# Two-layer block on one core: scores and first distances in pairs, two value groups side by side, values projected into the shared bank

## The reference

```
def _stablemax3_s(x):
    pos = 1.0 + x * (1.0 + 0.5 * x * (1.0 + x / 3.0))
    neg = 1.0 / (1.0 - x * (1.0 - 0.5 * x * (1.0 - x / 3.0)))
    return jnp.where(x >= 0, pos, neg)
qkv = layernorm(x) @ w_qkv.T
attn = stablemax3(q @ k.T * scale)               # per head
x = x + (attn @ v) @ w_out.T + b_out
logits = layernorm(x) @ router_w + router_b      # top 2 of 4 kept, made to sum to 1: gates
h = silu(xf @ w1[e]) * (xf @ w3[e])
x = x + sum_e gates[e] * (h @ w2[e])
```

## Time and profile before

| | us |
|---|---|
| median of three runs (1226.88 to 1228.73) | 1228.69 |
| the profiled execution | 1225.98 |
| its span in the trace | 1224.2 |
| PE busy in the span | 1143.0 (93%) |
| VectorE busy | 1041.6 (85%) |
| ScalarE busy | 1017.0 (83%) |
| GpSimd busy | 332.1 (27%) |

### The profile page before, as it was taken

How to read it: one execution, slowest core, us unless ns; L and a number is a source line. 1 busy time by engine, 2 the same in 40 slices (tenths; PEclk the granted TensorE clock), 3 DMA queues, 4 the chain that set the end, 5 groups by cost and what they waited for, 6 DMA issues and landing times.

```text
span 1224.2 us, 29210 instructions
## 1 busy us (share of the span) xinstructions
PE 1143.0 (93%) x10116; PEld 976.4 (80%) x10116; DVE 1041.6 (85%) x1998; ACT 1017.0 (83%) x1070; POOL 332.1 (27%) x707
## 2 busy tenths in 40 slices
PE   1567999999999999999999999999999999999988
PEld 1445888888888888888888888888888888898878
DVE  5777989888898988889898888989888889998833
ACT  1488988888998888899888889898888899888872
POOL 5113322212332222233222132322312233231111
PEclk9778999999999999999999999999999999999999
DMA  5111111222111122211112121111222111121000
GB/s 175 58 57 53 48 50 57 67 66 65 46 47 48 56 65 65 65 48 44 48 56 65 65 65 51 41 48 56 65 65 65 55 43 43 56 65 62 11 6 9
DMA packets 83689, 67.97 MB, mean 56 GB/s; under 512 B 6664, under 2 KB 82120, under 8 KB 83656
## 3 DMA queue, kind: packets, MB, share of 16 engines
q1 hardware_dynamic: 83080, 67.01, 17.1%
q10 hardware_dynamic: 576, 0.52, 0.2%
HBM read 45.42 MB, written 20.97 MB: 54 GB/s over the span
## 4 chain that ended last, share of the span: by engine, by line
PE 81%; DVE 5%; issue 4%; DMA 3%; SPq 3%; ACT 2%; POOL 2%; DVEq 0%; POOLq 0%; ACTq 0%
PE up_a L807 15%; PE up_a L983 10%; PE up_b L983 10%; PE up_b L807 9%; PE sc L876 9%; PE pv L823 7%; PE sc L966 6%; PE pv L807 5%; SPq L311 2%; DVE mx L716 2%; DVE y_acc L733 1%; DMA qk_scratch<-qk_split 1%; PE misc L1014 1%; PE misc L1015 1%; PE misc L938 1%
## 5 line engine op out<-in xcount | busy, mean ns | idle before, releaser
L464 ACT ACTIVATE w_sq<-sc 128x1024 f32<-128x1024 f32 x256 | 262.6, 1026 | 140.6 <-PE sc L876 133.6
L603 DVE SCALAR_TENSOR_TENSOR poly<-w_sq,sc 128x1024 f32<-128x1024 f32 x256 | 311.5, 1217 | 34.8 <-ACT w_sq L464 25.6
L716 DVE TENSOR_REDUCE mx<-sc 128x4 f32<-128x1024 f32 x256 | 305.1, 1215 | 18.0 <-PE sc L966 17.3
L521 ACT ACTIVATE poly<-poly,two 128x2048 f32<-128x2048 f32 x128 | 251.9, 1991 | 0.4
L526 ACT ACTIVATE poly<-poly 128x2048 f32<-128x2048 f32 x128 | 242.4, 1895 | 0.0
L876 PE MATMUL sc<-q_stack,k_pad 128*128 128x256 f32 x1024 | 179.1, 298 | 7.4 <-DVE poly L603 6.9
L472 ACT ACTIVATE silu_a<-up_a 128x512 f32<-128x512 f32 x256 | 154.0, 602 | 18.9 <-PE up_a L807 14.3
L876 PEld LDWEIGHTS sc<-q_stack,k_pad 128*128 128x128 f32 x1024 | 144.1, 193 | 25.0 <-issue 13.6
L807 PE MATMUL up_a<-xn_hi,w_hi 128*128 128x256 f32 x512 | 155.9, 304 | 6.2 <-DVE y_acc L733 1.3
L966 PE MATMUL sc<-k_pad,q_stack 60*128 60x256 f32 x1024 | 117.1, 329 | 31.7 <-DMA k_pad<-qk_scratch 22.9
L381 POOL TENSOR_TENSOR x_resb<-x_res,b_out_all 128x128 f32<-128x128 f32 x64 | 27.9, 457 | 431.8 <-DVE y_acc L656 361.4
(11 more groups left out here) (105 smaller groups left out, 2021.5 us busy)
## 6 DMA issues: line engine op xcount, KB each, us to landing
qk_scratch<-qk_split SPq DMA_DIRECT2D x32, 512.0 KB, 2.8
k_pad<-qk_scratch SPq DMA_DIRECT2D x256, 64.0 KB
q_stack<-qk_scratch SPq DMA_DIRECT2D x124, 128.0 KB
x_in<-in_L_attn_x_dram SPq DMA_DIRECT2D x32, 128.0 KB, 2.1
x_res<-in_L_attn_x_dram SPq DMA_DIRECT2D x32, 128.0 KB, 2.3
out_dram<-y_acc SPq DMA_DIRECT2D x32, 128.0 KB, 1.8
poly<-in_L_ffn_w_dram SPq DMA_DIRECT2D x2, 1024.0 KB, 7.2
q_stack<-m_split SPq DMA_DIRECT2D x64, 16.0 KB
```

The lines of the kernel that those rows point to most:

```text
L464: nc.scalar.activation(w_sq[:, u % 2, :], sc[:, u % 2, :], ACT.Square).then_inc(sq_ok, 1)
L521: nc.scalar.activation(poly[:, C * g:C * (g + 1), :], poly[:, C * g:C * (g + 1), :], ACT.Ln, bias=two[:]).then_inc(ln_ok, 1)
L603: nc.vector.scalar_tensor_tensor(poly[:, u, :], w_sq[:, u % 2, :], 3.0, sc[:, u % 2, :], ALU.add, ALU.mult).then_inc(poly_ok, 1)
L716: nc.vector.tensor_reduce(by_row[:, :, 2 * g:2 * g + 2], sc[:, u % 2, :].rearrange("p (j k t) -> p j k t", j=2, k=2), AX.X, ALU.min, negat ...
```

## The change

PE's order changes in five ways. (1) The scores go in pairs, u = (0, 1), (2, 3), (4, 5), (6, 7), and the first half of `down(0)` (its rows c = 0) goes ahead of the first pair. (2) `weighted_values` 0 and 1 stand side by side behind the last scores; before, group 0 stood behind `scores(4)`. (3) `router_logits` goes from between `scores(6)` and `scores(7)` to behind `up_a_unit(0)`, which is behind `maxima_T`, and `up_b_unit(0)` and `queries_operand` go ahead of `weighted_values(2)`. (4) `distances` 0 and 1 stand side by side, `weighted_values(3)` behind them. (5) The values are projected into `misc` instead of `pv`, straight behind `weighted_values(3)`, ahead of the units 1.

VectorE follows: `route_logits` goes from ahead of `scores_max(7)` to behind `add_expert(3)`, `add_expert(1)` goes behind `scores_max(3)`, and `queries_T` goes ahead of the router's comparisons. ScalarE does `square(1)` ahead of the copy of the attention output, the copy of the values before `silu(1)`, and the router's small exponential (L548) behind `weights_of(3)` instead of ahead of it. The number and the sizes of the operations stay the same.

The core of the diff:

```
@@ scalar, first half
                 silu(0)
                 square(0)
+                square(1)
                 if has(i, off - 1):
                     nc.scalar.copy(o_T[:], pv[:]).then_inc(o_ok, 1)
-                square(1)
-                silu(1)
-                square(2)
                 if has(i, off + 1):
...
-                                              pv[:, 0, c * D:(c + 1) * D].rearrange("p (h d) -> p h d", d=HD))
+                                              misc[:, c * D:(c + 1) * D].rearrange("p (h d) -> p h d", d=HD))
+                silu(1)
+                square(2)
                 silu(2)
@@ vector, second half
-                    if u == 6 and has(i, off - 1):
-                        route_logits()
-                    if u in (1, 2) and has(i, off - 2):
-                        add_expert(u - 1)
...
+                    if u in (1, 3) and has(i, off - 2):
+                        add_expert(u // 2)
                     if u == 4 and has(i, off - 1):
                         router_T()
...
+                if has(i, off - 2):
+                    add_expert(2)
+                if has(i, off + 1):
+                    split_maxima()
+                if has(i, off - 2):
+                    add_expert(3)
+                if has(i, off - 1):
+                    route_logits()
+                if has(i, off + 2):
+                    queries_T()
@@ tensor: units 0 to 7, weighted values
-                    pe.wait_ge(v_ok, n + 2 if has(i, off + 1) else n + 1)
+                    pe.wait_ge(v_ok, n + 1)
...
-                        pe.wait_ge(v_ok, m + 4)
...
+                    pe.wait_ge(o_ok, min(m + 2, B) if isinstance(i, int) else m + 2)
@@ tensor, first half
                 distance(0)
+                distance(1)
                 if has(i, off - 1):
                     weighted_values(i, off - 1, 3)
-                distance(1)
+                if has(i, off + 1):
+                    m = n + 1
+                    pe.wait_ge(qk_out, m + 1)
+                    for c in range(C):
+                        last = nc.tensor.matmul(misc[:, c * D:(c + 1) * D], xn_T[:, c * 128:(c + 1) * 128],
+                                                proj_T[:, 2, :], start=True, stop=True)
...
@@ tensor, second half: maxima_T, queries_operand, router_logits
                     if has(i, off - 1):
-                        pe.wait_ge(lg_ok, n)
+                        pe.wait_ge(xn2_out, n)
...
-                    if has(i, off + 1):
+                    if has(i, off - 1):
+                        pe.wait_ge(lg_ok, n)
+                    elif has(i, off + 1):
                         pe.wait_ge(m_ok, n + 2)
...
                     pe.wait_ge(xn2_out, m + 1)
+                    if has(i, off + 1):
+                        pe.wait_ge(m_ok, n + 2)
@@ tensor, second half: order
+                down(0, (0,))
+                score(0)
+                score(1)
+                down(0, (1,))
+                down(1)
+                score(2)
+                score(3)
+                down(2)
+                score(4)
+                score(5)
+                if has(i, off - 1):
+                    router_operand()
+                down(3)
+                score(6)
+                score(7)
                 if has(i, off):
+                    weighted_values(i, off, 0)
                     weighted_values(i, off, 1)
...
                 if has(i, off - 1):
                     up_a_unit(i, off - 1, 0)
+                    router_logits()
+                    up_b_unit(i, off - 1, 0)
+                if has(i, off + 2):
+                    queries_operand()
                 if has(i, off):
                     weighted_values(i, off, 2)
```

More of the change, by code:

```diff
@@ L543, in second_half @@
                         log_of(g + 1)
+                    if has(i, off):
+                        weights_of(g)
                     if g == G - 1 and has(i, off - 1):
@@ L548, in second_half @@
                         nc.scalar.activation(exp_l[:], shifted[:], ACT.Exp).then_inc(exp_ok, 1)
-                    if has(i, off):
-                        weights_of(g)
             act.wait_ge(consts_v, 4)
@@ L893, in first_half @@
                 distance(0)
+                distance(1)
                 if has(i, off - 1):
                     weighted_values(i, off - 1, 3)
-                distance(1)
+                if has(i, off + 1):
[4 more added lines that the diff above has]
+                                                proj_T[:, 2, :], start=True, stop=True)
+                    last.then_inc(v_full, 1)
                 ups(1)
                 distance(2)
-                if has(i, off + 1):
-                    m = n + 1
-                    after(pe, o_ok, n)
-                    for c in range(C):
-                        last = nc.tensor.matmul(pv[:, 0, c * D:(c + 1) * D], xn_T[:, c * 128:(c + 1) * 128],
-                                                proj_T[:, 2, :], start=True, stop=True)
-                    last.then_inc(v_full, 1)
                 ups(2)
@@ L969, in scores, with down @@
                     last.then_inc(s_full, 1)
-                def down(e):
+                def down(e, chunks=(0, 1)):
+                    if not has(i, off - 2):
+                        return
                     m = n - 2
@@ L980, in down @@
                         pe.wait_ge(acc_ok, E * C * m + C * (e - 1))
-                    for c in range(C):
+                    for c in chunks:
                         for f in range(FB):
```

39 lines of the change are left out of this document (4 added, 35 removed).

## The result

The changed kernel takes 1235.59 us (median of four runs, 1234.23 to 1236.74) against 1227.79 us for the kernel before in the same comparison (1226.77 to 1228.73). The ratio is 1.0063, with a 95% interval of 1.0046 to 1.0081: slower, by about 7.8 us. The profiled execution of the changed kernel took 1235.11 us, its span is 1233.4.

The account below looks back on a forecast made before the run. PE, nearly full but meeting VectorE at the last maximum, was taken as the bound. One step, 0 - 0.28 + 0.60 = +0.32 us, times 29 is +9.3; the start -1: +8.3, from 1228.69 to 1237.0 us; range 1227.5 to 1246.

Parts of the forecast that it names:

- the start: At n = 0 and n = 1, VectorE's waits amid the maxima go: -0.5 us each, -1 us in all.
- The head: Second half of a step up to the last maximum: its end comes 0.28 us earlier, bounds -0.40 and -0.15.
- rival 1: At the router transposes, POOL releases early: up to -0.62 us before the last maximum's end, 1223.3 us; chance 0.10.
- The tail: From the last maximum to the first `distances`: 0.60 us longer in each step, bounds 0.47 and 0.75.
- The first half: First half of a step, up to `up_b_unit(2)` behind `hidden(1)`: 0 us, between -0.17 and +0.1.
- Times 29: Steps n = 2 to n = 30: each costs +0.32 us, times 29 is +9.3 us.
- The end: End of the program, where ScalarE's exponentials set the pace: cost at 0.
- (2): Drains count in full: 5 boundaries of 0.19 us on PE each step, nothing waits, 1201 us; chance 0.02.
- (3): Gains and losses around the last maximum cancel, `up_b_unit(2)` no longer waits: 0.02 us a step, 1228.3 us; chance 0.11.
- (4): A new wait costed at 0 shows, such as at ScalarE's small exponential or copies: +0.3 us a step, 1246 us; chance 0.12.
- (5): The change as a whole doesn't do what it says; chance 0.

Follow-up runs that it names:

- The first experiment: The changed kernel with the router transposes behind `down(3)` and VectorE's copy of them behind `scores_max(5)`: 1228.32 us, ratio 1.0005 to the kernel before.
- the old start: The changed kernel with `weighted_values(0)` back behind `scores(4)` in n = 0 and n = 1 alone: 1235.73 us, ratio 1.0073 to the kernel before.

## Why the prediction was right

**The sign and the size.** Predicted +8.3 us, measured +7.8; for one step +0.32, measured +0.29. It came out by a sum whose terms were each a little off, and that it was met to 0.5 us is in part luck: the steps gave 7.2 us where the sum had 9.3, and the start did not give back the 1 us that the sum took off.

**The head: -0.28, measured -0.31.** The steps of the argument are all in the rows. The gap ahead of the first `down` is 0.17 us where 0.3 was forecast, but the first score comes 633.17 - 632.02 = 1.15 us behind `silu(7)`, as worked out (628.65 - 627.50). PE reaches the router transposes at 639.45 + 0.67 = 640.12, which is 8.10 us behind `silu(7)`; the prediction put it at 635.6 - 627.50 = 8.10. GpSimd ends `xn2` at 639.01 + 1.57 = 640.58, 8.56 behind `silu(7)`, exactly as before (636.06 - 627.50): its chain did not move. PE goes on at 640.71. From there to the end of the last maximum are 5.05 us, worked out as 5.07. So 0.2 us for each boundary between kinds of matmul carried the position to the tenth to which it was given. In the same timeline `down(1)`, with a score only behind it, takes 636.71 - 634.83 = 1.88 us to the next start, and `down(2)`, between scores, 639.45 - 637.47 = 1.98: 0.10 for the one more end, as counted. No run changes boundaries alone. PE's busy time does not show the price: it fell by 0.31 us a step and not by 1.0. Matmuls that follow each other start 0.12 us apart while each row is 0.28 long, so some 0.16 us of each wait lie under the row before it, an estimate from these rows; for the four waits that are new (first `down`, router transposes, logits, `up_b_unit(0)`) that makes 0.64, with the 0.31 about the 1.0 that was counted.

The -0.31 is a mean of two kinds of steps. In the step that the rows show, and from whose kind the prediction took its rows, the head fell by 0.24 (13.74 against 13.98), in the other kind by 0.38 (13.60), since GpSimd ends `xn2` 8.41 us behind `silu(7)` there instead of 8.55. The first experiment shows what waiting for GpSimd costs: without it the head is 13.32, that is 0.67 shorter than before. That is the -0.62 that rival 1 asked of an early GpSimd, and it would not have been early by itself.

The Trainium skill, "TensorEngine Tiling (Array Packing)", Key Properties, has the change of the tiling mode drain TensorE. The position of PE agrees that fewer changes save it time; the result shows that this saving is worth nothing where the next instruction in its queue waits for another engine.

**The tail: +0.60, measured +0.72.** This term and the next, both off by 0.12, were mis-sized most. The releases came as worked out: with E = 645.76, `split_maxima` ends at 646.79 + 0.41 = E + 1.44 and `add_expert(3)` at 647.13 + 0.59 = E + 1.96. But PE's rows start later than counted behind them: `router_logits` at 647.35, E + 1.59, `up_b_unit(0)` at 647.86, E + 2.10. Each wait thus costs 0.14 to 0.15 us from the end of the releasing row to the next start, where I took 0.1 and 0.05. The queries and keys come at E + 4.21, predicted E + 4.12. And the gain of 0.05 that I took off for VectorE's copy `xn_T` did not come: from the queries and keys to the first square are 651.61 - 649.97 = 1.64 us, before 5.07 - 3.47 = 1.60. (This step is of the longer kind, its tail is 5.85; the mean is 5.79.)

**The first half: 0, measured -0.12.** The step that failed is "it starts with PE's queries and keys and stays as it is". The chain of `hidden(1)` ran through `polynomial(1)`, and this waited in part for `square(1)`, behind ScalarE's copy. I looked mostly for what the new order could make late. My lower bound of -0.17 held it.

**Times 29.** The steps of the loop grew by 0.29 us each, 7.5 us for 26. The other three did not follow: n = 2 and 3 grew by 0.1 together, and n = 30, in which work for later batches is missing, fell by 0.4. So the product was 7.2, not 29 x 0.29 = 8.4.

**The start: -1, not settled.** The profiles give 82.4 and 84.2 before, 83.6 and 84.4 after: no gain, and a spread larger than the term. VectorE's waits at this place did not go away, they moved and grew. Its timeline before, n = 0 and n = 1, then after:

```profile
73.06 0.41 DVE L756 TENSOR_SCALAR m_split<-misc 16x256 fp32r<-16x256 f32 x1 [0.69 <-PE misc L999]
...
107.79 0.41 DVE L756 TENSOR_SCALAR m_split<-misc 16x256 fp32r<-16x256 f32 x1 [0.48 <-PE misc L999]
```

```profile
74.44 0.41 DVE L756 TENSOR_SCALAR m_split<-misc 16x256 fp32r<-16x256 f32 x1 [2.39 <-PE misc L999]
...
108.90 0.41 DVE L756 TENSOR_SCALAR m_split<-misc 16x256 fp32r<-16x256 f32 x1 [2.08 <-PE misc L999]
```

VectorE stood 1.22 and 1.11 us in the middle of the maxima before and 0.69 and 0.48 behind them, 1.91 and 1.59 in all; now it stands 0 and 0.38 in the middle and 2.39 and 2.08 behind, since both groups of weighted values are ahead of the transposed maxima. From the first maximum of the half to `split_maxima` it took 0.4 us longer at n = 0 and 0.1 at n = 1. I had named this and still taken half a microsecond of gain for each. The likelier value is 0. The end, also cost at 0, is 0.7 us longer in both profiles.

**The rivals.** GpSimd did not release early (rival 1): in both kinds of steps PE starts 0.13 to 0.14 us behind the end of `xn2`. But that GpSimd's rows are "the same in each step" was a wrong reading; in the kernel before, too, `xn2` ends 8.55 and 8.41 us behind `silu(7)` in turn. The saved boundaries did not come through (2): PE stood 0.48 us for GpSimd in this half, and 0.34 in the next. Head and tail did not cancel (3): the head and the first half came near its -0.28 and -0.17 (-0.31 and -0.12), but the tail was longer than the forecast had it, not shorter. Of the waits that I cost at 0 (4) one showed, VectorE's for `square(2)`, and it did not lengthen the step. The change does what it says (5).

Two small slips: with the stated bounds the lowest time is 1228.7 - 2.9 - 2.4 = 1223.4 us, not 1224; and the clock's row reads below 9 in three slices, the second to the fourth, not in four. Neither touches the forecast.

## What to carry over

Ahead of moving work out of an in-order queue, ask what the next waiting instruction in that queue waits for: the time saved is capped by that release, and all that is queued behind it is held too. A step that has to wait belongs behind work that covers its wait, and a step whose wait is only for a shared buffer should get columns of its own. Put a small step into a wait that is there in any case: taking the router logits ahead of the transposed maxima, and `up_b_unit(0)` back behind work, gave 20 us together.

## What the runs showed of the hardware

**Two kinds of steps.** After the change even and odd steps of the loop take 36.0 and 35.7 us, before 35.56 and 35.58. GpSimd's rows in two steps that follow each other:

```profile
638.62 0.20 POOL L409 TENSOR_TENSOR rstd<-rstd,newton 128x4 f32<-128x4 f32 x1 [0.22 <-POOL newton L402]
...
674.43 0.20 POOL L409 TENSOR_TENSOR rstd<-rstd,newton 128x4 f32<-128x4 f32 x1
```

In every other step GpSimd stands 0.22 us ahead of this row. The kernel before has the same (0.22 us ahead of the row at 634.10, none listed ahead of the one at 669.51). Before the change, and with the transposes behind `down(3)`, the head is the same in both kinds (13.98; 13.32). A delay on a lightly used engine (27% busy) was invisible as long as nobody waited for it. It accounts for 0.14 of the 0.31 us between the two kinds; 0.10 are in the tail and 0.08 in the first piece, and those are not explained. Why GpSimd stands in every other step is open.

**The start varies, and the end has two causes.** The start of the same kernel differed by 1.8 us between two profiles of before, and by 0.8 us for after. The end repeats within a kernel, 80.4 us twice before and 81.1 twice after, but differs between kernels: 81.1 us after, 82.4 with the old start, 84.4 with the transposes behind `down(3)`.

The first cause is the edit. In the last batch's turn there are no scores left. PE with the transposes behind `down(3)`, then after:

```profile
1194.88 0.38 PE L1025 MATMUL misc<-ident,xn 128*128 128x128 f32 x2
1197.36 0.36 PE L807 MATMUL up_a<-xn_hi,w_hi 128*128 128x256 f32 x1 [2.10 <-POOL xn_lo L428]
```

```profile
1204.74 0.38 PE L1025 MATMUL misc<-ident,xn 128*128 128x128 f32 x2
...
1207.23 0.36 PE L807 MATMUL up_a<-xn_hi,w_hi 128*128 128x256 f32 x1 [0.32 <-POOL xn_lo L428]
```

GpSimd ends `xn2` at 1192.70 in the one and at 1204.36 in the other. PE does the transposes 2.18 us behind it in the one, 0.38 in the other, and what follows hangs on them: here `down(3)` stands in front of the critical step, and that costs 1.8 us once. In the loop it fills a wait.

The second cause goes with the clock. The stretch from `silu(0)` to `silu(4)` of the last batch, first of the kernel with the old start, then of after, whose programs are the same there; the columns are the stretch, its length, busy us of PE, PEld, DVE, ACT and POOL with counts, the clock granted to PE, DMA share and GB/s:

```profile
1208.94:1216.88 7.94, 7.29 (x44) 6.94 (x45) 3.14 (x8) 2.39 (x5) 0.16 (x1) 0.79 0.00 0
```

```profile
1210.74:1217.40 6.66, 6.01 (x44) 5.59 (x45) 3.14 (x8) 2.39 (x4) 0.16 (x1) 1.00 0.00 0
```

The same 44 records of matmuls took 7.94 us at a mean granted clock of 0.79, which means 1.2 GHz for a part of the stretch, and 6.66 us at 2.4 GHz throughout. These 1.3 us are the difference of the two ends (82.4 and 81.1). With the transposes behind `down(3)` the stretch took 8.22 us at 0.68, 1.6 us more than in after, the rest of the 3.3. Why the clock fell there in the one kernel and not in the other is open.
